# An adaLN block on one core: two tiles of x ahead of the rest, and the first layer's gate weights loaded last with a group of row products of their own

## What is computed

```
mod = (silu(c) @ wmod) -> sa, ca, ga, sb, cb, gb          # 6 vectors of 512 per batch
h = layernorm(x) * (1 + ca) + sa
x = x + guard(ga) * (h @ (att_weight * keep_mask).T)       # 512 x 512 weights, 32 x 32 blocks kept or not
h = layernorm(x) * (1 + cb) + sb
x = x + guard(gb) * ffn(h)                                 # silu(h Wg' ag) * (h Wu' au), then Wd', 1376 inner
guard(g) = sign(g) * max(|g|, 0.25)
```

## Time and profile before

| | |
|---|---|
| Median of 3 runs | 173.75 us (173.65 to 174.42) |
| Profiled execution, device time | 174.27 us |
| Its span in the trace | 172.4 us |
| TensorE busy (matmul) | 166.0 us, 96% |
| VectorE, ScalarE, GpSimd busy | 111.4, 81.1, 30.1 us |
| First `linear` starts | 11.86 us after the span's start |

### The profile page before, as it was taken

How to read it: one execution, slowest core, us unless ns; L and a number is a source line. 1 busy time by engine, 2 the same in 40 slices (tenths; PEclk the granted TensorE clock), 3 DMA queues, 4 the chain that set the end, 5 groups by cost and what they waited for, 6 DMA issues and landing times.

```text
span 172.4 us, 2494 instructions
## 1 busy us (share of the span) xinstructions
PE 166.0 (96%) x856; PEld 127.3 (74%) x856; DVE 111.4 (65%) x229; ACT 81.1 (47%) x113; POOL 30.1 (17%) x38
## 2 busy tenths in 40 slices
PE   6979999999999999999999999999999999999992
PEld 6846554465478888888788888888888888888781
DVE  6787966993855999879775585447444312443584
ACT  3033005547999965875446624354334544252200
POOL 1143401950168410000000000008300000000000
PEclk9999999999999999999999999999999999999999
DMA  5999967999999602440000003002400000000015
GB/s 177 342 411 399 405 190 176 384 366 402 405 413 399 194 4 49 103 95 0 6 0 4 0 4 115 8 4 95 155 0 4 0 4 0 6 0 4 0 67 183
DMA packets 12775, 24.00 MB, mean 139 GB/s; under 512 B 3057, under 2 KB 5361, under 8 KB 12369
## 3 DMA queue, kind: packets, MB, share of 16 engines
q1 hardware_dynamic: 11040, 22.03, 35.3%
q10 hardware_dynamic: 1712, 1.66, 3.0%
HBM read 19.74 MB, written 2.11 MB: 127 GB/s over the span
## 4 chain that ended last, share of the span: by engine, by line
PE 90%; DVE 3%; DMA 3%; SPq 1%; issue 1%; ACT 0%; ACTq 0%
PE bank L998 46%; PE bank L1068 20%; PE bank L981 17%; DMA xt<-in_x 3%; PE bank L889 3%; PE bank L1054 2%; PE bank L960 2%; DVE xn L588 1%; SPq L286 1%; DVE xt L879 0%; DVE bns L574 0%; DVE xn L792 0%; DVE xt L870 0%; DVE xn L876 0%; PE bank L944 0%
## 5 line engine op out<-in xcount | busy, mean ns | idle before, releaser
L998 PE MATMUL bank<-ht,whi_gu 128*128 128x512 f32 x352 | 83.6, 391 | 0.0
L998 PEld LDWEIGHTS bank<-ht,whi_gu 128*128 128x128 f32 x352 | 65.5, 188 | 14.0 <-issue 0.8
L773 DVE SCALAR_TENSOR_TENSOR awork<-bank,scal,awork 128x512 f32<-128x512 f32 x22 | 16.5, 749 | 43.8 <-PE bank L998 40.1
L1068 PE MATMUL bank<-whi_dn,in_split 128*128 128x512 f32 x148 | 37.0, 389 | 0.0
L537 ACT ACTIVATE awork<-bank,scal 128x512 f32<-128x512 f32 x22 | 15.1, 688 | 45.0 <-PE bank L998 45.0
L1068 PEld LDWEIGHTS bank<-whi_dn,in_split 128*128 128x128 f32 x148 | 27.8, 188 | 5.8
L981 PE MATMUL bank<-awork,wffn 128*128 128x512 f32 x64 | 30.2, 602 | 0.2 <-ACT wffn L458 0.2
L480 ACT ACTIVATE whi_gu<-wffn 128x1024 fp32r<-128x1024 f32 x22 | 23.3, 1058 | 6.6 <-PE bank L998 6.6
L981 PEld LDWEIGHTS bank<-awork,wffn 128*128 128x128 f32 x64 | 11.0, 190 | 10.8 <-issue 9.3
L473 ACT ACTIVATE junk<-wffn 128x1536 uint8<-128x1536 uint16 x11 | 16.3, 1478 | 2.3 <-DMA wffn<-in_w_down 2.2
L782 DVE TENSOR_TENSOR in_split<-awork,in_split 128x512 fp32r<-128x512 f32 x21 | 15.5, 739 | 0.7
(11 more groups left out here) (80 smaller groups left out, 117.6 us busy)
## 6 DMA issues: line engine op xcount, KB each, us to landing
wffn<-in_w_gu SPq DMA_DIRECT2D x10, 512.0 KB, 9.6
modw<-in_mod_ln SPq DMA_DIRECT2D x6, 512.0 KB, 7.7
wffn<-in_w_down SPq DMA_DIRECT2D x10, 256.0 KB, 11.6
xt<-in_x SPq DMA_DIRECT2D x8, 256.0 KB, 6.7
modw<-in_mod_gate SPq DMA_DIRECT2D x2, 1024.0 KB, 12.8
maskt<-in_att_mask SPq DMA_DIRECT2D x4, 256.0 KB, 8.4
awork<-in_att_w SPq DMA_DIRECT2D x4, 256.0 KB, 8.5
modw<-in_mod_ln SPq DMA_DIRECT2D x1, 1024.0 KB, 6.8
```

What stands on the lines that cost most here:

```text
L773: dve.scalar_tensor_tensor(inner[:, s % 2, :], bank[gu_bank(s, 1)][:, :], scal[:, c, 1:2], silu_g[:, s % 2, :], ALU.mult, ALU.mult).then_i ...
L998: return pe.matmul(bank[gu_bank(s, u)][:, :], w, h, start=(k == 0 and part == 0), stop=(k == KT - 1 and part == 1))
L1068: last = pe.matmul(bank[4 + t][:, :], h, w, start=(c == 0 and part == 0), stop=(c == C - 1 and part == 1))
```

## The change

Two things move. In the opening only tiles 0 and 1 of x are loaded and treated first: their statistics, half normalisation, transposes and modulation (`modulate_pair`) come before tiles 2 and 3 are looked at, and TensorE does `linear(0, 0, 0)` and `linear(0, 0, 1)` before `rows_second`, the transposes of tiles 2 and 3 and `transposes(1)`. The gate weights are loaded last of the attention's loads, and their 16 products become a group of their own, `rows_gate`, with a `copy_rows` and `columns` of their own (`SETS` is 5). `linear(0, 1, 0)` and everything after it keep their order; in batch 1 the four `transposes` stand one `linear` later.

```diff
--- before.py
+++ after.py
-WARM_UP = 17
+WARM_UP = 15
-SETS = 4
+SETS = 5
+PAIR_XN = 2
+THIRD_XN = 6
...
@@ sync queue
-            for t in range(TT):
-                sp.dma_start(xt[:, t, :], x[t * P:(t + 1) * P, :]).then_inc(d_x[t], 16)
...
+            load_x(0)
+            load_x(1)
             load_mask(0)
             load_ln1(0)
             load_att(0)
+            load_x(2)
+            load_x(3)
             load_ln1(1)
...
             load_ln1(3)
-            sp.dma_start(modw[:, 2, :, :], mod_gate[0]).then_inc(d_gate[0], 16)
             load_mask(3)
             load_att(3)
+            sp.dma_start(modw[:, 2, :, :], mod_gate[0]).then_inc(d_gate[0], 16)
@@ gpsimd
             inverse_deviation(0, 0)
+            mask_weights(0)
             inverse_deviation(0, 1)
-            mask_weights(0)
@@ scalar
+            def modulate_pair():
+
+                act.wait_ge(xt_pair, 1)
+                act.wait_ge(modc_ok, 1)
+                for t, done in ((0, h_first), (1, h_second)):
+                    cols = slice(t * P, (t + 1) * P)
+                    act.activation(h1[:, 0, 0, cols], bank[4][:, cols], ACT.Identity,
+                                   bias=modc[:, 0, 0, 2:3], scale=modc[:, 0, 0, 0:1]).then_inc(done, 1)
...
-                part = slice(0, SEQ)
-                if n in FIRST_ALONE:
+                part = slice(0, SEQ) if n else slice(2 * P, SEQ)
+                if n and n in FIRST_ALONE:
...
             copy_rows(0)
+            modulate_pair()
+            copy_rows(1)
             modulate(0)
-            copy_rows(1)
             modulate(1)
             modulate(2)
             act.wait_ge(xn_ok, XN_FIRST + TT)
             move_first(act, BY_SYNC)
+            copy_rows(2)
             move_first(act, BY_SYNC + 1)
             move_first(act, BY_SYNC + 2)
-            copy_rows(2)
             move_first(act, BY_SYNC + 3)
             move_first(act, BY_SYNC + 4)
             modulate(3)
+            copy_rows(3)
+            modulate(4)
             copy_gate(0, bank[6])
-            modulate(4)
+            modulate(5)
             store_first_gate(act)
-            modulate(5)
@@ vector
-            for t in range(TT):
-                stats(0, t)
+            stats(0, 0)
+            stats(0, 1)
             sum_mask(0)
-            normalise_half(0, range(TT))
+            normalise_half(0, range(0, 2))
             keep_blocks(0)
             mod_columns(0)
-            normalise_half(1, range(TT))
+            stats(0, 2)
+            stats(0, 3)
+            normalise_half(1, range(0, 2))
+            normalise_half(0, range(2, TT))
+            normalise_half(1, range(2, TT))
             sum_mask(1)
...
             normalise(1)
+            sum_mask(3)
             keep_in_place(0)
+            keep_blocks(3)
             keep_in_place(1)
+            mod_columns(2)
             keep_in_place(2)
-            sum_mask(3)
-            keep_blocks(3)
-            mod_columns(2)
+            keep_in_place(3)
             gate_sums()
             guard_first_gate()
-            keep_in_place(3)
             transpose_first(0)
-            gate_linear(0, 0)
-            gate_linear(0, 1)
             transpose_first(1)
-            gate_linear(0, 2)
-            gate_linear(0, 3)
+            for t in range(TT):
+                gate_linear(0, t)
             transpose_first(2)
             transpose_first(3)
@@ tensor
             def rows_third():
                 pe.wait_ge(d_ln1[3], 16)
-                pe.wait_ge(d_gate[0], 16)
                 pe.wait_ge(rows_copied, 2)
                 pe.wait_ge(keep_ok, 2)
-                mod_rows([(v, ln1_block(3, v)) for v in range(2)] +
-                         [(GATE_AT + i, modw_block(2, i)) for i in range(KT)], bank[6])
+                mod_rows([(v, ln1_block(3, v)) for v in range(2)], bank[6])
+
+            def rows_gate():
+                pe.wait_ge(d_gate[0], 16)
+                pe.wait_ge(rows_copied, 3)
+                mod_rows([(GATE_AT + i, modw_block(2, i)) for i in range(KT)], bank[6])
...
+                if b == 0 and k == 0 and t == 1:
+                    pe.wait_ge(h_second, 1)
+                elif t == (2 if b == 0 and k == 0 else 1 if alone else 0):
                     pe.wait_ge(h_ok, TT * b + k + 1)
...
             transposes(0, (0, 1))
             columns(0)
-            transposes(0, (2, 3))
-            transposes(1)
 
             between = {
-                (0, 0): [rows_second],
-                (0, 1): [lambda: columns(1), lambda: mask_blocks(1)],
-                (0, 2): [lambda: transposes(2)],
+                (0, 1): [rows_second, lambda: transposes(0, (2, 3)), lambda: transposes(1),
+                         lambda: columns(1), lambda: mask_blocks(1)],
+                (0, 3): [lambda: transposes(2)],
                 (1, 1): [lambda: mask_blocks(2), lambda: transposes(3)],
-                (2, 1): [rows_third, lambda: mask_blocks(3)],
-                (2, 2): [lambda: columns(2)],
-                (3, 0): [gate_first],
+                (2, 0): [rows_third, lambda: mask_blocks(3)],
+                (2, 1): [lambda: columns(2)],
+                (2, 3): [rows_gate],
+                (3, 0): [lambda: columns(3)],
+                (3, 2): [gate_first],
             }
```

More of the change, by code:

```diff
@@ L221, in adaln_block @@
         xt_done = sem("xt_done")
+        xt_pair = sem("xt_pair")
         h_first = sem("h_first")
+        h_second = sem("h_second")
         h_ok = sem("h_ok")
@@ L430, in copy_rows @@
                     act.wait_ge(consts_ok, 5)
-                if n == 3:
-                    act.wait_ge(cols_done, 1)
-                act.activation(rows[:, n % 3, :], bank[2 if n == 3 else 6][:, 0:P], ACT.Identity,
+                if n >= 3:
+                    act.wait_ge(cols_done, n - 2)
+                act.activation(rows[:, n % 3, :], bank[2 if n == SETS - 1 else 6][:, 0:P], ACT.Identity,
                                bias=onerow[:, 0:1]).then_inc(rows_copied, 1)
@@ L446, in modulate @@
                 act.wait_ge(xt_done, n + 1)
-                act.wait_ge(modc_ok, SETS if layer else SET_OF[k] + 1)
+                act.wait_ge(modc_ok, SETS - 1 if layer else SET_OF[k] + 1)
                 if q < 2:
@@ L516, in _ @@
             check_chunk(next(check_at))
-            copy_rows(3)
+            copy_rows(SETS - 1)
             check_chunk(next(check_at))
@@ L831, in _ @@
             normalise(2)
-            mod_columns(3)
+            mod_columns(SETS - 1)
             split(8)
@@ L929, in columns @@
                 else:
-                    pe.wait_ge(keep_ok, [1, 1, KT][n])
+                    pe.wait_ge(keep_ok, [1, 1, KT, KT][n])
                     if n:
@@ L950, in transposes @@
                 dst = bank[4 + n % 2] if q == 0 else bank[n % 2]
-                if k == 0:
-                    pe.wait_ge(xn_ok, XN_FIRST + TT * q if q else TT)
+                if n == 0:
+                    pe.wait_ge(xn_ok, PAIR_XN if TT - 1 not in tiles else THIRD_XN)
+                elif k == 0:
+                    pe.wait_ge(xn_ok, XN_FIRST + TT * q)
                 if n == 2:
@@ L961, in transposes @@
                                         ident[:, :])
-                if TT - 1 in tiles:
-                    last.then_inc(xt_done, 1)
+                last.then_inc(xt_done if TT - 1 in tiles else xt_pair, 1)
             def linear(b, k, t):
@@ L969, in linear @@
                     pe.wait_ge(h_first, FIRST_ALONE.index(k) + 1)
-                if t == (1 if alone else 0):
+                if b == 0 and k == 0 and t == 1:
+                    pe.wait_ge(h_second, 1)
+                elif t == (2 if b == 0 and k == 0 else 1 if alone else 0):
                     pe.wait_ge(h_ok, TT * b + k + 1)
@@ L1003, in gate_up_first @@
                 pe.wait_ge(wgu_hi, 1)
-                pe.wait_ge(modc_ok, SETS)
+                pe.wait_ge(modc_ok, SETS - 1)
                 pe.wait_ge(h_ok, 11)
@@ L1167, in _ @@
                         columns(SETS - 1)
-                    if (k, t) == (2, 0):
+                    if (k, t) == (2, 1):
                         transposes(8)
                         transposes(9)
-                    if (k, t) == (2, 1):
+                    if (k, t) == (2, 2):
                         transposes(10)
```

## The result

| | before | changed |
|---|---|---|
| Median | 173.67 us (6 runs, 173.35 to 174.42) | 175.75 us (6 runs, 174.25 to 175.88) |
| Ratio, with its 95% interval | | 1.0085 (1.0053 to 1.0117) |
| Profiled execution, its span | 174.27, 172.4 us | 174.41, 172.6 us |
| First `linear` starts | 11.86 | 10.29 |
| First `gate_up` starts | 48.77 | 49.10 |

The change makes the kernel slower: the forecast was 173.6, its range ended at 174.6, and slower had a chance of 0.14. The changed kernel's six times fall into two groups: 174.25 and 174.41 (the profiled one), and four from 175.72 to 175.88. A later repeat of the same kernel gave 1.0042 (1.0012 to 1.0072). So two things are to be explained: a loss of about 0.4% that comes back in the repeat, and the upper group. The first `gate_up` is read from the chain, where it starts as the last `linear` ends.

The account below looks back on a forecast made before the run. TensorE was taken as the bound from the first `linear` on. The terms -1.06 + 0.66 + 0.44 - 0.22 gave -0.18 us, with 0 to 0.3 of new waits: median 173.75 to 173.6, range 173.0 to 174.6.

Parts of the forecast that it names:

- What bounds the kernel: TensorE is the bound from the first `linear` at 11.86 to the last product.
- The start: Opening: ln1(0) lands at 8.1 instead of 9.36, so the first `linear` starts at 10.5, 1.35 us earlier.
- landing-does-not-move rival: Opening: ln1(0) still lands at 9.36, first `linear` stays at 11.8; 0.88 us slower, 174.6; chance 0.07.
- What the early start buys: Up to `rows_second`: one `linear` pulled ahead (0.86) and 0.2 from an earlier group; about 0.3 lost waiting for ln1(2); gain 1.06.
- the moved transposes and the restart: Behind `rows_second`: six transposes add 0.66 us; a `linear` behind a group takes 1.06 instead of 0.86.
- Waits that could open: VectorE followed through the new order, then gate, ScalarE and second layer norm: 0 to 0.3 us of small new waits.
- -1.06 + 0.66 of the opening: Opening: 1.06 us gained by the earlier first `linear`, against 0.66 for six transposes moved onto TensorE's path.
- The places that I called thin: Mask sum 1: nothing or 0.1 late; mask sum 3: nothing to spare; `modulate(4)`: thinnest, at 30.9; second layer norm: 0.7 to spare.
- The stall of 0.22: Ahead of `linear(0, 3, 0)`, a 0.22 us wait for the modulation of feature block 3 goes in the new order.
- A new wait in the middle: Gate sums hold `modulate(4)`, late mask sums hold `mask_blocks(1)` and `mask_blocks(3)`, or second layer norm late: 0.7 to 1.2 us; chance 0.07.
- The clock: Ahead of the first `linear` TensorE's clock falls to half speed for 5 us, losing 2.5: 176.1; chance 0.01.
- the gate's 0.22: Gate's own group: 0.44 us for extra row products and `columns(3)`, less 0.22 for a wait ahead of `linear(0, 3, 0)`.

Follow-up runs that it names:

- the gate part alone: Changed kernel with the opening of before put back and 17 warm-up products, so only the gate's loads, group and order differ from before: 174.05 us, 1.0022.
- the swapped one: Changed kernel with 17 warm-up products and GpSimd's `mask_weights(2)` ahead of batch 1's second inverse deviation: 174.51 us, 1.0047.
- profile 1: First of six more profiled executions of the unedited changed kernel: 174.62 us.
- profile 2: Second of six more profiled executions of the unedited changed kernel: 174.54 us.
- its two variants: Changed kernel with 17 warm-up products instead of 15 (174.69 us, 1.0041), and with three filler products ahead of the first `linear` (174.57 us, 1.0045).
- the early flag: VectorE's `flag_vector(2)`, for TensorE's load near 83 us, moved ahead of the first `transpose_blocks`: changed kernel 174.44 us (15 warm-ups), 174.57 (17); kernel before 173.59, 173.57.
- the opening-only kernel: Kernel before with the opening by two tiles alone, 17 warm-up products and the gate's products in the third group as before: 174.32 us, 1.0032.

## Why the prediction was wrong

**What bounds the kernel.** Right for the profile before, whose chain is TensorE's alone from 11.86 on (ahead of it TensorE also waited 0.3 us for normalised x, which I left out). Not for the changed kernel: there the chain runs over the load of x, VectorE and GpSimd until 21.43, and TensorE is the bound from `linear(0, 2, 0)` on.

**The start.** The landing of ln1(0) moved as forecast: TensorE waited for it until 8.03 in the first profile (I had 8.1), and the first `linear` came at 10.29 (10.5). The landing-does-not-move rival is dead: no profile of the new opening, whatever else was edited, had its first `linear` later than 10.83. The size was right too: eight profiles of the unedited changed kernel have their first `linear` at 10.14 on average, five with before's opening at 11.55, 1.4 us between them (I had 1.35). The profile that I worked from was a late one, 11.86, where the four others have 11.38 to 11.62, but batch 1's first tile was late in it too.

**What the early start buys.** `rows_second` at 12.53 with a wait of 0.25, where I had 12.7 to 12.8 and 0.3. TensorE was 0.45 us ahead at `linear(0, 1, 0)` (16.92 against 17.37); my terms made it 0.40. The terms for the moved transposes and the restart hold.

**Waits that could open: the step that failed.** I wrote "I followed VectorE through the new order" and stopped at the mask sums. I followed the masks whose sums had moved, 1 and 3, and the gate. I did not follow mask 2 and batch 1, whose code did not move, though TensorE was to come there 0.4 us sooner. In the trace of before, the weights of block 2 were ready at 21.07 and were wanted at 21.42, and VectorE ahead of them had waited 0.68 us for a landing that the change doesn't touch. The slack there was 0.35 us from the multiply's end, 0.2 once the 0.15 us between that end and TensorE's start (21.28 to 21.43 in the profile after) is taken off; the lead was 0.38. In the three other profiles with all of before's order the first of these two slacks was 0.42, 0.42 and 0.01, so it was never much over the lead. So the whole -1.06 + 0.66 of the opening, a term of -0.40 in my sum, came out as nothing, and what was left of the sum was 0.22, with a restart 0.32: the 0.33 us between the two first `gate_up`.

The lead doesn't only end there, the floor also rose. GpSimd's pair ahead of it, the inverse deviation and the multiply, took 1.70 us from start to end in three of the four profiles with all of before's order (1.99 in the fourth, and 1.99 with the gate part alone), and 1.83 to 2.01 in every changed kernel but the swapped one. VectorE's first tile of batch 1 began on average at the same time (14.32 in the four, 14.31 in the eight unedited changed ones), but the weights of block 2 were ready at 21.19 in place of 20.86. Of these 0.33 us the pair is 0.20 (1.97 against 1.77), and profile 1's wait for mask 2 is the rest (1.1 us in one of eight). In the profile after, the longer one of the pair is the inverse deviation, 1.00 in place of 0.71. The length goes with when VectorE's normalisation starts: 0.14 to 0.21 us behind the inverse deviation in the three profiles with 1.70, 0.09 behind in the two with 1.99, and from 0.09 ahead to 0.01 behind in the eight (1.84 to 2.01). It stands behind `keep_blocks(2)`, which needs TensorE's `mask_blocks(2)`, so an earlier TensorE starts it sooner (19.19 in place of 19.51). That is a correlation: no run moves the normalisation alone, and with the fallen clock, where it started 0.46 behind, the pair still took 1.91.

The first `gate_up` comes at 49.01 on average in the eight and at 48.57 in the four, 0.44 us, and what follows it is 0.1 us longer on average, which is the flag. So some 0.5 of the 0.75 us between the medians (174.58 and 173.83) is seen in profiles. The rest I can't place.

**The places that I called thin.** `mask_blocks(1)`: right, a wait of 0.23 for VectorE's sum in two profiles (17 warm-ups, and profile 2), none in the others. `mask_blocks(3)`: a wait in the swapped kernel alone. `modulate(4)` and the second layer norm: no wait in any profile. `mask_blocks(2)`, which I had not named, waited 0.47 in profile 1 for the late mask 2. The stall of 0.22 went as forecast.

**The rivals.** "A new wait in the middle" is the one that came nearest: its 174.4 to 175.0 holds the medians of the repeat and its two variants (174.58, 174.69, 174.57), but it named other places. I gave it a chance of 0.07 to pass half a per cent, on the places that I had followed. (The three chances for slower add up to 0.15 and the one for faster is 0.06, where my last line on them has 0.14 and 0.07.) The repeats are just inside that bound (1.0042), the first series is beyond it.

**The clock.** With 12 warm-ups it falls as that rival says. In the profiled execution of the changed kernel with 15 and the early flag it fell too. Its stretches (start and end, length, busy time of PE, PEld, DVE, ACT and POOL with counts, granted clock, DMA share, GB/s):

```profile
10.00:11.00 1.00, 0.23 (x1) 0.23 (x2) 0.96 (x4) 0.74 (x2) 0.15 (x1) 1.00 0.99 393
11.00:12.00 1.00, 1.00 (x2) 0.43 (x2) 0.93 (x4) 0.07 (x1) 0.00 (x0) 0.50 1.07 412
...
13.00:14.00 1.00, 1.00 (x2) 0.00 (x0) 1.00 (x4) 0.00 (x0) 0.00 (x0) 0.50 1.06 397
14.00:15.00 1.00, 1.00 (x25) 0.69 (x28) 0.86 (x2) 0.00 (x0) 0.00 (x0) 0.80 1.05 385
```

The granted clock is 0.50, which is 1.2 GHz, from about 11, just behind the start of the first `linear` at 10.77, until about 14.4 (worked out from the 0.80 of the last row), and the first four records take 3.60 us in place of 1.99:

```profile
10.77 3.60 PE L1007 MATMUL bank<-awork,wffn 128*128 128x512 f32 x4 [0.82 <-ACT wffn L453]
```

It costs 1.6 us where it strikes, not the 2.5 that I worked out, and with 12 warm-ups part of that vanishes at the same floor: the first `linear` came at 9.88 and the first `gate_up` at 49.47, 0.5 after the average of 49.01. What TensorE did before it fell was 15 (or 12) warm-ups, 16 row products' records and three small products, with waits of 0.35 (0.52 with 12) and 0.82 us. No profile with 17 shows it. Over whole executions the granted clock was 0.99 or less in one of 12 of either kernel with 15 warm-ups and the early flag, and in most of those with 12. The Trainium skill (TensorE: Matmul & The Clock Gate, The HAM clock gate) says that an idle TensorE falls back to 1.2 GHz; in these profiles it fell with no wait over 0.9 us since the warm-up, so my reading of the trace, that a gap of 1.0 us does not do it, was taken from one execution and is not a rule.

**The upper group stays open.** Of 24 executions of the unedited changed kernel in three series, seven took 175.5 to 175.9. Their granted clock was 0.997 to 1.000, and in the profile of 15 warm-ups with a fallen clock it was 0.99, so it isn't that. No execution with the flag early and a clock of 0.996 or more passed 175.01 (23 of the changed kernel), which speaks for the late flag, which cost up to 1.2 us; but the changed kernel with 17 warm-ups and the late flag had none above 175.02 in 12 either. Six more profiles met none.

## What to carry to other kernels

When a change lets the bound engine come earlier, list what it will ask for next in order, and for each the slack in the trace of before: the time between ready and wanted. The first place whose inputs come from a load that the change leaves in its place is where the lead ends, and the gain is that slack at most. Work added ahead of that place vanishes in the same wait (with six transposes moved there, 0.66 us, the opening-only kernel reached its first `gate_up` 0.08 later), and work added behind it is paid in full (the gate's 0.22). And take the slacks from more than one execution: here four profiles had 0.35, 0.42, 0.42 and 0.01.

## What was not expected

The load at the head of that chain waits for bandwidth, as I read it. From 10 to 14 us the mean busy share of the 16 DMA engines stands at 0.99 to 1.07 with 385 to 418 GB/s in the three profiles in which I read it, and the landings around it follow each other at 0.66 to 0.70 us for 256 KB in the profiles before and after. So a tile lands by the bytes ahead of it, and reordering the loads behind which it stands moved nothing on average (14.32 and 14.31). The Trainium skill (DMA: Bandwidth & Descriptors, Where 436 GB/s comes from) gives 435 GB/s as what the 16 ports into SBUF can take; the trace is 4 to 12% below it. Not tried: batch 1's first tile of x ahead of ln1(1) or of attention weights 1, which is what these rows suggest.

Between executions of one program the first `linear` moved by 1.5 us (9.25 to 10.78 in eight profiles), and the first `gate_up` by 1.1 (48.41 to 49.54).
